# Two calls of a routed expert layer: each gather of rows also waits for the gather two places ahead of it

## The reference

```python
gate_weights = jax.nn.softmax(x @ gate_W + gate_b)
topk_vals, topk_idx = jax.lax.top_k(gate_weights, 2)
boost = x
for i in range(2):
    eo = selected_expert(boost, topk_idx[:, :, i])   # relu(boost @ W1[e] + b1[e]) @ W2[e] + b2[e], hidden 256
    outs.append(eo)
    if i < 1:
        boost = boost + 0.5 * eo
fused = sum(topk_vals[:, :, i:i + 1] * outs[i] for i in range(2))
x = layer_norm(x + fused)
```

## Time and profile before

| | |
|---|---|
| median of 3 executions | 2140.37 us |
| all three | 2141.48, 2134.65, 2140.37 us |
| span of the profiled execution | 2178.4 us |
| its mean granted TensorE clock | 0.921 of full speed |
| call 0 of `experts_0`, from its first gather to the first gather of call 1 | 1034.36 to 1119.10 us |
| call 1, to the first instruction behind it on GpSimd | 1119.10 to 1193.48 us |

### The profile page before, as it was taken

How to read it: one execution, slowest core, us unless ns; L and a number is a source line. 1 busy time by engine, 2 the same in 40 slices (tenths; PEclk the granted TensorE clock), 3 DMA queues, 4 the chain that set the end, 5 groups by cost and what they waited for, 6 DMA issues and landing times. The chain is left out here.

```text
span 2178.4 us, 35417 instructions
## 1 busy us (share of the span) xinstructions
PE 1866.1 (86%) x11556; PEld 1497.2 (69%) x11556; DVE 1597.3 (73%) x4179; ACT 1237.1 (57%) x2908; POOL 543.2 (25%) x602
## 2 busy tenths in 40 slices
PE   8999999999999999984766486999889998962772
PEld 6888888888888888873656344777667766741662
DVE  7999999999999999976546475777467765767524
ACT  6888888888888888864444363333233322440333
POOL 0111111111111111110544502444034421000472
PEclk9999999999999999996879587999999999985796
DMA  7000000000000000013554100000000000022354
GB/s 226 1 1 1 1 1 1 1 1 1 1 1 1 1 1 1 1 36 56 99 95 105 52 1 1 0 0 0 1 0 0 0 0 5 2 58 87 85 99 92
DMA packets 64893, 61.06 MB, mean 28 GB/s; under 512 B 10698, under 2 KB 54708, under 8 KB 64612
## 3 DMA queue, kind: packets, MB, share of 16 engines
q1 hardware_dynamic: 52276, 41.50, 6.5%
q0 software_dynamic: 10384, 16.59, 4.9%
q10 hardware_dynamic: 2080, 1.05, 0.2%
HBM read 40.12 MB, written 18.73 MB: 27 GB/s over the span
## 5 line engine op out<-in xcount | busy, mean ns | idle before, releaser
L461 DVE TENSOR_TENSOR probT<-turn_ps,probT 128x512 fp32r<-128x512 f32 x512 | 335.3, 686 | 63.3 <-ACT probT L359 63.2
L374 ACT ACTIVATE prob<-prob,negmax 128x512 f32<-128x512 f32 x512 | 375.4, 740 | 4.6 <-DVE negmax L455 4.6
L176 POOL TENSOR_TENSOR x<-x,scaled 128x512 f32<-128x512 f32 x128 | 166.8, 1303 | 802.1 <-DVE scaled L476 802.1
L455 DVE CUSTOM_DVE_ANT_0 prob<-score_ps,bias 128x512 f32<-128x512 f32 x512 | 341.2, 685 | 6.9 <-issue 1.1
L359 ACT CAST probT<-turn_ps 128x512 fp32r<-128x512 f32 x512 | 284.0, 598 | 21.7 <-PE turn_ps L259 21.7
L259 PE MATMUL turn_ps<-ident,prob 128*128 128x128 f32 x2048 | 266.2, 273 | 1.3 <-DVE probT L461 1.1
L276 PE MATMUL work_ps<-probT,val 128*128 128x512 f32 x1024 | 257.2, 393 | 0.1
L259 PEld LDWEIGHTS turn_ps<-ident,prob 128*128 128x128 f32 x2048 | 236.7, 140 | 28.2 <-DVE probT L461 3.4
L247 PE MATMUL score_ps<-k,q 64*128 64x512 f32 x1536 | 213.8, 410 | 2.4 <-DVE negmax L455 2.1
L276 PEld LDWEIGHTS work_ps<-probT,val 128*128 128x128 f32 x1024 | 187.5, 188 | 39.9 <-DVE probT L461 1.7
L247 PEld LDWEIGHTS score_ps<-k,q 64*128 64x128 f32 x1536 | 135.4, 185 | 47.3 <-issue 19.7
(11 more groups left out here) (510 smaller groups left out, 4010.5 us busy)
## 6 DMA issues: line engine op xcount, KB each, us to landing
ew<-L_ffn_fc_weight SPq DMA_DIRECT2D x32, 256.0 KB
bias<-bias_line SPq DMA_DIRECT2D x16, 448.0 KB, 8.4
mid_rows<-row SPq DMA_DIRECT2D x40, 128.5 KB
last_rows<-row SPq DMA_DIRECT2D x40, 64.0 KB
rows_dram<-qk SPq DMA_DIRECT2D x1, 2304.0 KB, 18.5
x_rows<-x SPq DMA_DIRECT2D x4, 512.0 KB, 7.1
acc_dram<-zero POOLq DMA_DIRECT2D x1, 2048.0 KB, 16.3
out<-x SPq DMA_DIRECT2D x4, 512.0 KB
```

The lines of the kernel that those rows point to most:

```text
L176: pool.tensor_tensor(mine, mine, scaled[a][:, :, :], ALU.add).then_inc(added, 1)
L374: act.activation(mine, mine, ACT.Exp, bias=negmax[p % 2][:, i, a:a + 1], scale=-1.0, accum_out=total[p % 4][:, i, a:a + 1]).then_inc(exp_d ...
L455: dve.tensor_tensor_reduce(prob[p % 2][a][:, i, :], score_ps[i % 2][a][:, :], bias[:, h, first:first + SEQ][:, ::-1], -1.0, 3.0e38, ALU.ad ...
L461: dve.tensor_tensor(probT[1][:, g % QT, :], turn_ps[g % 2][:, :], probT[0][:, g % QT, :].bitcast(F32), ALU.subtract).then_inc(turned_lo, 1)
```

## The change

Before each gather from the third on, GpSimd also waits until the gather two places ahead of it has landed, so that no more than two gathers are in flight. `gathered[before % X_RING]` counts 16 for each landing in that buffer, and the value waited for is the one of the landing of gather n - 2. It holds for both calls. No instruction is added to another engine, removed or moved: the order of instructions on every engine is as before.

```diff
                 r = n % X_RING
                 if n >= X_RING:
                     pool.wait_ge(row_ready, n - X_RING + 1)
+                if n >= 2:
+                    before = n - 2
+                    pool.wait_ge(gathered[before % X_RING], 16 * (before // X_RING + 1))
                 pool.indirect_dma_start(out=xg[r][:, :], out_offset=None, in_=table,
                                         in_offset=bass.IndirectOffsetOnAxis(ap=source[:, i, n:n + 1], axis=0)).then_inc(gathered[r], 16)
```

## The result

The change made the kernel slower. In the comparison that first timed it the changed kernel took 2182.05 us (median of 4, 2180.33 to 2183.99) against 2137.51 us (2132.53 to 2141.48) for the kernel before: 44.5 us more, a ratio of 1.0211 [1.0196, 1.0226]. The forecast was 2142 us, with 2150 as its upper end.

The account below looks back on a forecast made before the run. The prediction held that gathers come early and TensorE waits for them only at the calls' ends; 0.5 + 0.6 + 0.5 + 0.2 = 1.8 us on the timed 2140.37 us gave 2142 us, range 2135 to 2150.

Parts of the forecast that it names:

- step 1: Start of both calls: the third gather now waits for the first, with TensorE waiting; 0.5 us.
- step 2: Middle of first call: L = 3.3 caps the pitch at 1.85 us against 1.744, partly hidden by lead; 0.6 us.
- L: Time from a gather's start to its last packet; taken as 3.3 us in the first call's middle, 2.6 in the second.
- step 4: Second call: cap of 1.5 us hidden under a pitch of 1.643 us; only its last tiles cost, 0.2 us.
- lead of 1.75 us: Middle of first call: the 19th gather is usable 1.75 us before its use, so that much delay costs nothing.
- step 3: Last tiles of first call: slow 7.5 us landings are a queue that two in flight keep busy; 0.5 us, 0 to 3.
- step 5: Given back: fewer gathers might let row stores and last gathers through earlier; at most 5.7 us, taken as 0.
- The landing becomes the pace: Rival, first call's middle: L rises to 4.2 us with two in flight and delay feeds itself; 2152 us, chance 0.13.
- L over 3.7 us or an end stretch moved by more than 3 us: Signs of being wrong: L with two in flight over 3.7 us, or either end stretch moving over 3 us.
- Stores profit: Rival: all 5.7 us of waits for stores and last gathers come back; 2136.5 us, chance 0.10.
- the wait hardly ever bites: Rival: L falls to 3.0 us with two in flight and only the start costs, 0.5 us; 2141 us, chance 0.18.
- last tiles lose their overlap: Rival, first call's end: the 7.5 us is each gather's latency, not queue; 11.7 us more, 2152 us, chance 0.07.

Follow-up runs that it names:

- swapped waits: Changed kernel with the landing's wait written ahead of the finished row's: 2167.75 us, 1.0139 against the kernel before, 12.2 us faster than the change.
- forty buffers: Changed kernel with 40 buffers for gathered rows, so no gather waits for a finished row: 2170.88 us, 1.0150 against the kernel before.
- 2185 comparison: One of five comparisons in which the unchanged kernel before took 2180 to 2190 us; in the one meant here the change took 2195.91 us, 1.0067.
- 2137 comparisons: The two comparisons in which the unchanged kernel before took about 2137 us; the change took 2182.05 and 2179.96 us there.
- three in flight: Changed kernel waiting for the gather three places ahead instead of two: 2143.37 us, 1.0027 beside before at 2136.93; 2179.48 us, 0.9989 beside 2180.69.
- second comparison: Before at 2136.93 us, timed beside the change again (2179.96 us), a wait three places ahead (2143.37), waits in other order (2167.75) and 40 buffers (2170.88).
- one in flight: Changed kernel with each gather waiting for the landing of the one directly ahead: 2329.73 us, 1.0672 against the kernel before.

## Why the prediction was wrong

**Start of both calls (step 1, 0.5 us): right.** The third gather starts 2.98 us after the first in both calls, 0.26 us later than before in call 0 (2.72) and 0.48 us in call 1 (2.50), 0.7 us together.

**Middle of call 0 (step 2, 0.6 us): failed, at "the wait itself I cost at nothing" and "a waiter goes on 0.4 us behind the last packet".** L was a little high (3.3 taken, 2.97 measured), and the 0.4 us for TensorE was right in most places (where a gather's last packet was a straggler it was up to 1.6). GpSimd, with a `row_ready` wait ahead of the landing's, goes on 0.70 us later still. The cap is (2.97 + 0.4 + 0.70) / 2 = 2.04 us, not 1.85, and the measured pitch is 48.9 / 23 = 2.13 us. The swapped waits and the forty buffers show this term by itself, in two ways. The Trainium skill, "DMA: Bandwidth & Descriptors", section "Anatomy of one DMA — SWDGE (gpsimd) path", gave the prediction an estimate of 2.15 us for this transfer; the trace differs, with a median of 3.0 us to landing. Neither number holds the waiter's lag, which was the missing term.

**Call 1 (step 4, 0.2 us): failed by the same term.** L = 2.6 was right (2.59). The cap is (2.59 + 0.4 + 0.70) / 2 = 1.85 us where 1.5 was written, measured 44.1 / 23 = 1.92 us. That is over any pitch read for this call, so nothing was hidden.

**The pitches that the caps were held against: failed, and this is the larger part of the miss.** 1.744 and 1.643 us, and with them the lead of 1.75 us, came from an execution of 2178.4 us, while the timed ones took 2137. The prediction saw the 38 us and wrote that "the calls are 7% of the span, so the term carries over unscaled". It is no scaling: a good part of the 38 us lay in the calls themselves and made the slack against which the new wait looked free. How the two failures share the miss: with the lag alone put right in the prediction's own sum, the caps are (3.3 + 0.4 + 0.70) / 2 = 2.20 and (2.6 + 0.4 + 0.70) / 2 = 1.85 us, and 23 x (2.20 - 1.744) - 1.75 = 8.7 us, 28 x (1.85 - 1.643) - 2 = 3.8 us and 1.2 us for its other terms make 13.7 us, 2154 us. That is near what the 2185 comparison shows (15.2 us). The other 28 us or so are the slack that wasn't there in the 2137 comparisons (43.0 and 44.5 us). There the two calls of the change take 33.6 us more than those of three in flight (174.2 and 140.6, by the starts on GpSimd), and three in flight is 6.4 us over before. Where before spends its 2137 us can only be worked out: in the second comparison before's time less the 1.9 us by which a time exceeds its span, less the mean 1035.7 us ahead of the calls, 116.2 us of the stage behind and 851.6 us of the rest in the four profiles of this comparison, leaves 131.5 us for its calls, against 174.2 us for the change. This 131.5 us is not profiled, it takes for granted that before is like its relatives outside the calls, and the parts that it subtracts vary by up to 5 us among the four.

**Last tiles (step 3, 0.5 us): right.** The queue reading held. With two in flight the last packet of a gather of row 0 comes after 3.2 to 5.5 us, not 7.5, and with one in flight, where each is alone, after 3.2 us. The packets of the last seven take from 1101.4 to 1119.8, 18.3 us, against 17.1 in the profile of before: 1.3 us more, within the step's 0 to 3. (By the starts on GpSimd, the 33rd to the 40th take 17.5 us against 12.7, since the last ones are now issued later.)

**Given back (step 5, 0): right.** VectorE's waits for a row's store are gone from the calls, 3.5 us, and the time isn't seen to gain by it: it waits for tiles instead.

**The rivals.** "The landing becomes the pace" is what happened, and its mark (gathers 10 to 33 over 46 us; they took 48.9) was the right one. Its mechanism wasn't: L did not rise to 4.2 us. The 0.70 us on GpSimd came in its place, which with L = 2.97 makes 3.67, about the 3.7 us from which that rival counted; and its 2152 us still leaned on the same slow pitch. That a mark came true whose mechanism didn't is luck. The prediction's own signs of being wrong, L over 3.7 us or an end stretch moved by more than 3 us, did not show: they looked at the transfers and not at the waiter. "Stores profit" and "the wait hardly ever bites" are refuted, and so is "last tiles lose their overlap".

**What stays open.** Why the kernel before takes 2137 us in some comparisons and 2180 to 2190 us in others (it isn't the number of the chip: chip 5 gave both), and how before looks at 2137 us. By the profiles of its relatives some 28 us of it lie in the calls and some 14 in the stage behind (116 us in the 2137 comparisons, 127 to 139 in the others). Why TensorE's signals come late in the longer kind, and by far more while gathers are issued in one unbroken run, is open too.

## What to carry to other kernels

Before you use slack that a profile shows, hold its span against the timed runs. If it is longer, find in which stretch, for slack in such a stretch may not exist in the runs that count. Price a wait for a transfer as start to use plus the waiter's own lag, divided by the transfers in flight, and compare that with the pitch that the rest could keep, not with the one it keeps now; with two in flight instead of three this kernel lost 1.7% (2179.96 against 2143.37 us). And where an instruction has two waits, put the one that ends last first: it was worth 12 us of 43 here. With three in flight in a 2185 comparison, where the landing was hardly ever the last to come, the same swap was worth nothing (2180.13 against 2179.48 us).

## What the runs showed of the hardware

- A gather on GpSimd whose landing wait stands behind a wait for a row starts 0.69 to 0.72 us after TensorE's use of the same landing; with that wait first, or alone, 0.21 to 0.22 us from the ninth gather on. For a wait for a row it is 0.27 us as the first of two or alone and 0.75 us as the second. The second wait stands as an instruction of its own in the trace.
- Forty gathers issued without a pause (1.25 us apart) cost 1.9% in two comparisons; TensorE, ScalarE and VectorE stand for 4 to 13 us at a time although the queue has no backlog, and where it was looked up (1056.23 in call 0) the signal that releases them comes 2.7 us behind the matmul's modelled end.
- The 0.95 us row of a gather on GpSimd ends well before its data land (median 3.0 us). The Trainium skill, "Perfetto Trace Analysis", section "DMA Instruction — SWDGE (GPSIMD)", says that such a window ends with the generation of descriptors and not with the data. The trace agrees that the data land later; what the engine does in the window it doesn't show.
- In the trace of the changed kernel the waits that are put down to the row are waits on a landing. An example, a transpose and the gather behind it, from call 0:

```profile
1093.33 0.33 PE L862 MATMUL x_ps<-ident,xg 128*128 128x128 f32 x1 [1.22 <-DMA xg<-x_rows,source]
```

```profile
1094.03 0.94 POOL L853 DMA_INDIRECT xg<-x_rows,source  x1 [1.55 <-DVE row L951]
```

The gather is charged to `row`, yet it starts 0.70 us behind the use of the landing, as all the others do that waited for one. No gather of either call starts less than 3.1 us after the end of the row whose buffer it takes, so none waited for its row: the 22.2 us charged to `row` in the list near the top are waits for landings too.
